# Attention's output summed as 64 by 375 beside the queries, and picked places of two tiles moved to PSUM, in a one-core audio tower on Trainium2

## The reference

```python
q = (x @ Wq).reshape(b, n, HEADS, DIM) * DIM ** (-0.5)
kv_scores, indices = _pk(x, Wq_pk, pk_keys)
k = jnp.einsum('bnhk,bnhkd->bnhd', kv_scores, keys_table[ind])
v = jnp.einsum('bnhk,bnhkd->bnhd', kv_scores, values_table[ind])
sim = jnp.where(causal, jnp.einsum('bihd,bjhd->bhij', q, k), neg)
attn = jax.nn.softmax(sim, axis=-1)
out = jnp.einsum('bhij,bjhd->bhid', attn, v)
return out.transpose(0, 2, 1, 3).reshape(b, n, HEADS * DIM) @ Wo
```

## Time and profile before

| | us |
|---|---|
| median of 3 runs (lowest, highest) | 6795.9 (6795.37, 6803.57) |
| the profiled execution, its own time | 6795.46 |
| its span | 6793.6 |
| PE, busy | 5417.7 |
| POOL, busy | 4478.9 |
| DVE, busy | 3201.8 |
| ACT, busy | 2089.3 |
| mean granted TensorE clock of the span | 0.718 |

### The profile page before, as it was taken

How to read it: one execution, slowest core, us unless ns; L and a number is a source line. 1 busy time by engine, 2 the same in 40 slices (tenths; PEclk the granted TensorE clock), 3 DMA queues, 4 the chain that set the end, 5 groups by cost and what they waited for, 6 DMA issues and landing times.

```text
span 6793.6 us, 88054 instructions
## 1 busy us (share of the span) xinstructions
PE 5417.7 (80%) x24336; PEld 3758.2 (55%) x24336; DVE 3201.8 (47%) x14095; ACT 2089.3 (31%) x4501; POOL 4478.9 (66%) x4574
## 2 busy tenths in 40 slices
PE   2668788887978878787878878787788878788867
PEld 1446556555656556565655656565565656555533
DVE  6534644544464453445454344545534454640156
ACT  0224233332423332232323223232323324232332
POOL 2676767767676776767677676767677676767300
PEclk9667677766767776676777677676767767676767
DMA  1211111111111111111111111111111111111000
GB/s 44 73 51 47 53 45 53 52 46 51 43 53 44 53 52 48 51 44 53 43 53 49 48 53 44 53 43 53 46 51 53 43 53 45 52 47 53 24 22 12
DMA packets 166417, 321.92 MB, mean 47 GB/s; under 512 B 81980, under 2 KB 90772, under 8 KB 165710
## 3 DMA queue, kind: packets, MB, share of 16 engines
q0 software_dynamic: 144384, 295.20, 15.1%
q1 hardware_dynamic: 21166, 20.00, 1.1%
q10 hardware_dynamic: 288, 0.07, 0.0%
HBM read 310.37 MB, written 4.61 MB: 46 GB/s over the span
## 4 chain that ended last, share of the span: by engine, by line
POOL 34%; PE 29%; DVE 15%; issue 15%; ACT 4%; DMA 3%; DVEq 0%; POOLq 0%; SPq 0%; ACTq 0%
POOL store L427 34%; PE gath L613 9%; DMA store<-in,idx_now 3%; PE accu L475 2%; PE dense L467 2%; PE work L636 2%; DVE mx L1359 2%; PE gath L663 1%; PE sims L655 1%; DVE idxf L1299 1%; DVE picks L1295 1%; PE work L595 1%; PE work L690 1%; DVE prob_odd L1356 1%; PE work L648 1%
## 5 line engine op out<-in xcount | busy, mean ns | idle before, releaser
L427 POOL DMA_INDIRECT store<-in,idx_now x4512 | 4457.6, 988 | 1773.8 <-issue 1349.3
L613 PEld LDWEIGHTS gath<-wbd,store 128*128 128x128 f32 (+1 forms) x9024 | 1598.1, 272 | 804.1 <-issue 658.5
L613 PE MATMUL gath<-wbd,store 128*128 128x8 f32 (+1 forms) x9024 | 1591.1, 314 | 508.2 <-DMA store<-in,idx_now 500.1
L887 ACT ACTIVATE past<-dense,edge 128x375 bf16<-128x375 f32 x1024 | 588.2, 574 | 1613.7 <-PE dense L462 1613.4
L475 PE MATMUL accu<-dense_w,store 128*128 128x375 f32 x2048 | 1029.0, 591 | 33.0 <-ACT dense_w L895 33.0
L467 PE MATMUL dense<-parts_f,hot 128*128 128x375 bf16 x3072 | 819.5, 384 | 47.4 <-ACT dense_w L895 45.1
L895 ACT ACTIVATE dense_w<-dense 128x375 f32<-128x375 f32 x1024 | 495.5, 484 | 275.4 <-PE dense L468 260.2
L475 PEld LDWEIGHTS accu<-dense_w,store 128*128 128x128 f32 x2048 | 455.0, 237 | 136.8 <-issue 91.8
L467 PEld LDWEIGHTS dense<-parts_f,hot 128*128 128x128 bf16 x3072 | 317.7, 109 | 366.9 <-issue 274.0
L462 PE MATMUL dense<-ranksT,hot 128*128 128x375 bf16 x1008 | 379.6, 377 | 70.5 <-ACT past L887 70.3
L468 PE MATMUL dense<-past,far 128*128 128x375 bf16 x1024 | 397.6, 388 | 0.0
(11 more groups left out here) (276 smaller groups left out, 6685.3 us busy)
## 6 DMA issues: line engine op xcount, KB each, us to landing
store<-in,idx_now POOLq DMA_INDIRECT x4512, 2.5
x_in<-in SPq DMA_DIRECT2D x16, 187.5 KB
store<-in SPq DMA_DIRECT2D x1, 2048.0 KB, 8.9
queries_kept<-n3T SPq DMA_DIRECT2D x16, 93.8 KB, 2.3
h_saved<-h SPq DMA_DIRECT2D x16, 93.8 KB
store<-queries_kept SPq DMA_DIRECT2D x16, 93.8 KB, 2.3
store<-h_saved SPq DMA_DIRECT2D x16, 93.8 KB
out<-store SPq DMA_DIRECT2D x16, 93.8 KB
```

The source lines that it names most:

```text
L427: nc.gpsimd.indirect_dma_start(rows[0:slots, r * PER + i, :], None, kv_table, bass.IndirectOffsetOnAxis(ap=idx_now[0:slots, at:at + 1], ax ...
L613: last = mm(gath[:, 0, at:at + 8], rows[0:slots, r * PER + i, :], wbd[0:slots, t * GATHERS + n, :], start=True, stop=True)
L887: fn(past[:, n % 2, :], dense[:, 0, 0:S], ACT.Relu, bias=edge[:, 0:1]).then_inc(s["dense_u"], 1)
```

## The change

The mix of attention now has the 64 columns of `vo` as the stationary side and the transposed probabilities as the moving side: three matmuls of 375, 250 and 125 columns that sum into `work[D:128, 0]`, the upper partitions of the bank whose lower ones hold the queries. The blocks of the probabilities are transposed in another order to suit it. At the end ACT copies the 64 by 375 sum to `oT` and PE transposes it back, three blocks of 64 by 125, into `work` bank 1, where DVE's residual add reads it. `last_outputs` moves to `work` bank 1, after `mix(5)`, and PE waits for ACT's copy of it there. The wait for `h2_done` moves from the first row group to `turn_picks` of tile 2. `gath` is then free in attention; `take_inside` could take rows there, but `GROUPS_INSIDE` is eight zeros. Places of tiles 0 and 2 move to PSUM (`sims` bank 0 and `gath`), for which the gradient's results in `sims` bank 0 go to the upper half of `work` and to `work` bank 0. The fill lists take nine groups in `turn` rather than five, and one fewer in three places of `FILL_GRADIENT` and in the last entry of `FILL_SECOND`.

```diff
-FILL_TURN = ((0, 3), (0, 2))
+FILL_TURN = ((0, 5), (0, 4))
-FILL_GRADIENT = ((3, 2), (0, 1), (0, 1), (0, 1), (2, 2))
+FILL_GRADIENT = ((3, 1), (0, 1), (0, 0), (0, 1), (2, 1))
-FILL_SECOND = ((11, 6), (7, 5))
+FILL_SECOND = ((11, 6), (7, 4))
+GROUPS_INSIDE = (0,) * H
...
+        oT = two_q[D:128, 0:S]
-        place_banks = (places_s[:], sims[0:P, 0], places_s[:])
+        place_banks = (sims[0:P, 0], sims[0:P, 0], gath[0:P, 0])
-        PAIRS = [(0, 0, 0), (1, 0, P), (1, 1, 2 * P), (2, 0, 0), (2, 1, P), (2, 2, 2 * P)]
+        BLOCKS = [(0, 0), (0, P), (1, 0), (0, 2 * P), (1, P), (1, 2 * P)]
...
+                if t == 2:
+                    pe.wait_ge(s["h2_done"], b + 1)
...
-                if g == 0 and t == 0:
-                    pe.wait_ge(s["h2_done"], b + 1)
...
-                        last = mm(work[0:P, 0, j * D:(j + 1) * D], kvT[D:128, H - 1, tile(j)], wo_s[D:128, H - 1, :],
+                        last = mm(work[0:P, 1, j * D:(j + 1) * D], kvT[D:128, H - 1, tile(j)], wo_s[D:128, H - 1, :],
...
                 def mix(h):
                     pe.wait_ge(s["pT_done"], b * H + h + 1)
-                    if h == H - 1:
-                        pe.wait_ge(s["vo_done"], b * (NT + 1) + NT + 1)
-                    for c, (i, j, at) in enumerate(PAIRS):
-                        last = mm(gath[0:P, 0, i * D:(i + 1) * D], pT[:, c // 3, at:at + P], vo[:, j, h * D:(h + 1) * D],
-                                  start=(h == 0 and c == 0), stop=(h == H - 1 and c == 5), skip_group_check=True)
+                    for j in range(NT):
+                        last = mm(work[D:128, 0, j * P:S], vo[:, j, h * D:(h + 1) * D], pT[:, min(j, 1), (0, 0, 2 * P)[j]:(S, 2 * P, S)[j]],
+                                  start=(h == 0 and j == 0), stop=(h == H - 1 and j == NT - 1), skip_group_check=True)
...
                     if h + 1 < H:
                         scores(h + 1)
-                    if h + 1 == H - 1:
-                        last_outputs()
                     if h + 2 < H:
                         queries(h + 2)
+                    if following:
+                        take_inside(b + 1, GROUPS_INSIDE[h])
                     dense_steps(b, STEPS_A[h])
                     if h >= 1:
                         mix(h - 1)
+                    if h + 1 == H - 1:
+                        last_outputs()
+                        pe.wait_ge(s["vo_done"], b * (NT + 1) + NT + 1)
...
-                mix(H - 1).then_inc(s["o_mm"], 1)
+                mix(H - 1).then_inc(s["turned_mm"], 1)
+                pe.wait_ge(s["half_done"], b * (H + 1) + H + 1)
+                for t in range(NT):
+                    last = tr(work[0:P, 1, t * D:(t + 1) * D], oT[:, tile(t)], ident[D:128, D:128])
+                last.then_inc(s["o_mm"], 1)
...
-                mm(sims[0:D, 0, 0:S], mlrb[:], n3T[:], start=True, stop=True).then_inc(s["x0_mm"], 1)
+                mm(work[D:128, 0, 0:S], mlrb[:], n3T[:], start=True, stop=True).then_inc(s["x0_mm"], 1)
-                mm(sims[0:D, 0, 0:S], w1T_s[:], dz[:, 1, :], start=True, stop=True).then_inc(s["dx_mm"], 1)
+                mm(work[D:128, 1, 0:S], w1T_s[:], dz[:, 1, :], start=True, stop=True).then_inc(s["dx_mm"], 1)
...
-                    if h + 1 == H - 1:
-                        act.wait_ge(s["vo_mm"], b * (NT + 1) + NT + 1)
-                        nc.scalar.copy(vo[:, :, (H - 1) * D:], work[0:P, 0, 0:NT * D].rearrange("p (j d) -> p j d", d=D)).then_inc(s["vo_done"], 1)
...
                     if h == H - 2 and soften_next is not None:
                         soften(*soften_next)
+                    if h + 1 == H - 1:
+                        act.wait_ge(s["vo_mm"], b * (NT + 1) + NT + 1)
+                        nc.scalar.copy(vo[:, :, (H - 1) * D:], work[0:P, 1, 0:NT * D].rearrange("p (j d) -> p j d", d=D)).then_inc(s["vo_done"], 1)
...
+                act.wait_ge(s["turned_mm"], b + 1)
+                nc.scalar.copy(oT, work[D:128, 0, 0:S]).then_inc(s["half_done"], 1)
...
                 v.tensor_tensor(h2[:].rearrange("p t d -> p (t d)"), h1_now[:].rearrange("p t d -> p (t d)"),
-                                gath[0:P, 0, 0:NT * D], ALU.add).then_inc(s["h2_done"], 1)
+                                work[0:P, 1, 0:NT * D], ALU.add).then_inc(s["h2_done"], 1)
```

More of the change, by code:

```diff
@@ L130, in tower @@
         mlrb = sb("mlrb", [D, D])
-        mblr_s = sb("mblr_s", [D, 1])
+        mblr_s = sb("mblr_s", [128, 1])
         params = sb("params", [D + 1, 2, D])
@@ L626, in fill, with take_inside @@
                         dense_steps(b, 1)
+            def take_inside(b, n):
+                for _ in range(n):
+                    take_group(b, 0, at_group[0])
+                    at_group[0] += 1
             def attention(b, turned_picks, following):
@@ L684, in attention @@
                         mix(h - 1)
+                    if h + 1 == H - 1:
+                        last_outputs()
+                        pe.wait_ge(s["vo_done"], b * (NT + 1) + NT + 1)
                     pe.wait_ge(s["s_norm"], b * H + h + 1)
-                    for c, (i, j, at) in enumerate(PAIRS):
+                    for c, (half, at) in enumerate(BLOCKS):
                         if c == 3:
                             dense_steps(b, STEPS_B[h])
-                            pe.wait_ge(s["half_done"], b * H + h + 1)
-                        last = tr(work[0:P, 1, at:at + P], prob[h % 2][:, c // 3, at:at + P], ident[0:P, 0:P])
+                            pe.wait_ge(s["half_done"], b * (H + 1) + h + 1)
+                        last = tr(work[0:P, 1, c % 3 * P:(c % 3 + 1) * P], prob[h % 2][:, half, at:at + P], ident[0:P, 0:P])
                         if c == 2:
@@ L721, in gradient @@
                     for t in range(NT):
-                        tr(sims[0:P, l, t * D:(t + 1) * D], (x0, x1)[l][0:D, tile(t)], ident[0:D, 0:D])
-                        last = tr(sims[0:P, l, 192 + t * D:192 + (t + 1) * D], dz[:, l, tile(t)], ident[0:D, 0:D])
+                        dst = (work[0:P, 0], sims[0:P, 1])[l]
+                        tr(dst[:, t * D:(t + 1) * D], (x0, x1)[l][0:D, tile(t)], ident[0:D, 0:D])
+                        last = tr(dst[:, 192 + t * D:192 + (t + 1) * D], dz[:, l, tile(t)], ident[0:D, 0:D])
                 last.then_inc(s["t_mm"], 1)
@@ L734, in turn @@
             def turn(b):
+                if isinstance(b, int) and b == 0:
+                    take_inside(0, sum(GROUPS_INSIDE))
                 turn_ranks(b)
@@ L1041, in gradient @@
                 between()
-                fn(sg[:, 2, :], sims[0:D, 0, 0:S], ACT.Sigmoid, bias=mblr_s[:, 0:1]).then_inc(s["alr_done"], 1)
+                fn(sg[:, 2, :], work[D:128, 0, 0:S], ACT.Sigmoid, bias=mblr_s[D:128, 0:1]).then_inc(s["alr_done"], 1)
                 nc.scalar.copy(n3T[:], sims[0:D, 1, 0:S]).then_inc(s["mq_done"], 1)
@@ L1049, in gradient @@
                 act.wait_ge(s["t_mm"], b + 1)
-                for l in range(2):
-                    nc.scalar.copy(xt[:, l, :, 0:D], sims[0:P, l, 0:192].rearrange("p (t d) -> p t d", d=D))
-                    last = nc.scalar.copy(dzt[:, l, :, :], sims[0:P, l, 192:384].rearrange("p (t d) -> p t d", d=D))
+                for l, src in enumerate((work[0:P, 0], sims[0:P, 1])):
+                    nc.scalar.copy(xt[:, l, :, 0:D], src[:, 0:192].rearrange("p (t d) -> p t d", d=D))
+                    last = nc.scalar.copy(dzt[:, l, :, :], src[:, 192:384].rearrange("p (t d) -> p t d", d=D))
                 last.then_inc(s["t_done"], 1)
@@ L1057, in turn @@
             def turn(b):
+                fill(b, 0, sum(GROUPS_INSIDE))
                 keep_ranks(b)
@@ L1415, in gradient @@
                 dve.wait_ge(s["dx_mm"], b + 1)
-                v.tensor_tensor(g2, g2, sims[0:D, 0, 0:S], ALU.add).then_inc(s["g1_done"], 1)
+                v.tensor_tensor(g2, g2, work[D:128, 1, 0:S], ALU.add).then_inc(s["g1_done"], 1)
                 dve.wait_ge(s["g1_done"], b + 1)
```

9 lines of the change are left out of this document (4 added, 5 removed).

## The result

The changed kernel takes 6783.2 us (median of 7, 6776.52 to 6788.48), the kernel before, run beside it, 6803.57 us (median of 7). The ratio is 0.9966, 95% interval 0.995 to 0.9981. The forecast was 6820 us, slower; the sign was wrong, the time lies inside the range. The profiled execution took 6788.39 us (span 6786.6), about the slowest of its seven, and the one of before was about the fastest, so the two traces differ by 7 us only where the medians differ by 20.

The account below looks back on a forecast made before the run. Each 391.8 us cycle was taken as bound by POOL's gathers, then the path through attention to POOL's restart. Terms -82 + 10 + 24 + 42 + 30 = +24 us gave 6820 us, range 6765 to 6856.

Parts of the forecast that it names:

- Part 1, places: Tile 0's places in PSUM stop DVE holding up POOL's gathers: -5.5 us per batch, 15 times, -82 us.
- part (1): Stretch of the cycle from POOL's restart to the end of the last row group: 274.7 us, set by POOL.
- Part 5, fills: Four dense steps instead of three behind the last row group: +1.9 us per batch, 16 times, +30 us.
- The cover of 28.3 us: PE's idle time waiting for rows in part (1), expected to hide the delay from row groups moved ahead, costed at 0.
- Part 4, the end: Copy, three transposes and add between mix(7) and turn_picks of tile 2: +2.6 us per attention, 16 times, +42 us.
- part (4): Stretch of the cycle from attention's last mix to POOL's restart: 6.3 us, on the path, near 9 after the change.
- Parts 2 and 3, mix and head 6: In attention: the wide mix +0.6 us (+10 in all); head 6's wait for ACT's copy +1.5, nothing hides it (+24).
- part (2): Stretch of the cycle from the last row group to the next attention: 9.7 us, near 11.5 after the change.
- forecast (A): Whole kernel: the lengthened tail beats the freed gathers, 6820 us, slower; chance 0.48.
- C: Whole kernel: no change, the two sides cancel, 6795 to 6809 us; chance 0.15.
- rival B: Attention's end: denser mix keeps the clock at 2.4 GHz longer, half of 8.9 us won in 14 attentions, 6758 us; chance 0.2.
- D: PE falls behind in part (1), its 28.3 us of idle time go, slower still at 6865 us; chance 0.12.

Follow-up runs that it names:

- p1_places: The kernel before with only tile 0's places moved to PSUM and the gradient's banks moved out of their way; ratio 0.9876 to the kernel before.
- p2_fills: The kernel before with only the change's four new fill lists; ratio 1.006 to the kernel before.
- p4_undo_places: The changed kernel with the places of tiles 0 and 2 back in SBUF, all else kept; ratio 1.0104 to the kernel before.
- p5_wait: The kernel before with only the last head's projection moved behind mix(5) and PE's wait for its copy; old mix kept; ratio 1.0084 to the kernel before.
- r_after_warm: The changed kernel with ten matmuls that nothing reads added in PE's waits of heads 6 and 7; ratio 0.9899 to the kernel before.
- p8_warm: p1_places with ten matmuls that nothing reads added in PE's waits of heads 6 and 7; ratio 0.9874 to the kernel before.
- r_tail0: p1_places with FILL_SECOND changed so that no dense step stands between a batch's last row group and attention; ratio 0.9819 to the kernel before.
- p9_tail0: The same kernel as r_tail0, timed on an occasion when every kernel took 9.1 to 9.4 ms; ratio 0.9981 to the kernel before.
- p3_mix: The kernel before with the new mix, its end, head 6's wait and the moved wait for h2_done, without places and fills; ratio 1.0086 to the kernel before.
- r_inside3: The changed kernel with three row groups of the next batch summed in heads 5 to 7 of attention, tile 2's places in SBUF; 6434.09 us, ratio 0.9445.
- r_both: r_inside3 with FILL_SECOND changed so that no dense step stands behind the last row group; 6379.72 us, ratio 0.936 to the kernel before.

## Why the prediction was wrong

By its own terms, per cycle, from the means of the two profiles. The forecast's terms make +1.1 us, the measured ones -1.8:

- **Part 1, places: right, 0.9 too small.** Forecast -5.5, measured -6.4 in part (1), and -6.2 in p1_places alone; by ratios 84 to 94 us where 82 stood. One slip: it was counted 15 times, and there are 14 cycles that can gain. The stretch of batch 1's picks lies ahead of the first attention, which starts at 502.5 us in both traces, and the last part (1) had no slow picks already before (268.4 us, after 268.8).
- **Part 5, fills: near.** Forecast +1.9, measured +1.4 here and +2.4 in p2_fills. The cover of 28.3 us held.
- **Part 4, the end: right in the sum, in part by luck.** Forecast +2.6, measured +2.8. In the cycle shown above turn_picks starts 2.0 us behind the last mix's modelled end, where it started 0.2 ahead of it: +2.2. The three transposes took 0.5 us, not 0.8. The rest of the 2.8 is that part (4) too comes in kinds: in the kernel before it was 6.3 us in the cycle that the forecast took, and 8.8 where the turning of the picks ran at 1.2 GHz (rows below, granted clock 0.50).
- **Parts 2 and 3, mix and head 6: the step that failed.** The mechanism was right and the terms were mis-sized: +0.6 and +1.5 were forecast, and attention grew by 0.4 in all. First, at clocks that are alike it grew by 1.3 (p2_fills to p4_undo_places). The wait is 1.1 to 1.2 of that (p5_wait), because head 7 takes 0.65 us back: "nothing hides it" was wrong. The mix is the remaining 0.1 or 0.2: in the middle of attention one head's period rose from 8.75 to 9.05 us and the next one's fell from 9.70 to 9.39. Second, the clock, which the terms left as it was: in the changed kernel 7 of 12 attentions have a tail above 0.75, one had before. The four of them without a dip take 98.3 us, the four with a lower tail and no dip 99.95. 1.7 us in more than half of the cycles are worth some 15 us.

Busy time behind two attentions of the kernel before (columns as above; the clock is 0.78 and 0.50):

```profile
3747.00:3753.00 6.00, 6.00 (x43) 4.99 (x42) 2.07 (x6) 2.86 (x7) 0.00 (x0) 0.78 0.01 1
4136.00:4145.00 9.00, 9.00 (x42) 7.54 (x41) 2.06 (x6) 3.50 (x8) 0.02 (x1) 0.50 0.00 1
```

Against the shorter attentions stands that the changed kernel has more dips (5 for 3). The four terms with their measured sizes make -6.4 + 1.4 + 0.4 + 2.8 = -1.8 us per cycle. When batch 14's attention starts the changed kernel is 16 us ahead; then there is no slow pick left to win on, and it loses 9 of them, some 4 in the last two attentions (92.1 and 88.9 us against 90.8 and 86.3) and 4 in part (2) between them (8.1 against 4.3). That is the 7 us between the traces.

So neither the forecast (A) nor C decided alone: the sum was off by 2.9 us per cycle, 1.7 of them in attention, 0.9 in the places and 0.5 in the fills, less 0.2 at the end; and rival B, which had the faster sign, had its mechanism there in part. It put the gain at half of 8.9 us, 4.45, in every attention; it is 1.7 in seven of twelve, 1.0 on the mean. The rule of the Trainium skill that it leaned on (TensorE: Matmul & The Clock Gate, Part 1: activity of the array releases the gate) agrees with r_after_warm and p8_warm, where added matmuls go with a higher tail (0.82 for 0.77, 0.73 for 0.60). That the denser mix is enough is not borne out by p4_undo_places, whose mix is the wide one and whose tail is 0.60. **Open:** what decides between dip and no dip, and between the two tails. The same matmuls gave both: a place of picks or a fill list switched it, and so did another occasion with the same kernel (r_tail0 and p9_tail0). That the wide mix lifts the tail is not shown, only that the changed kernel and p3_mix have it and p4_undo_places has not.

D fell: PE's waits for rows are still 28.9 us. And the model of the whole, that POOL's stall between its restarts is what the cycle can win, held best: r_inside3 and r_both won 5.5 and 6.4% on the kernel before by it.

## What to carry to other kernels

Move one operand of long elementwise VectorE work to PSUM where a GpSimd queue issues indirect DMAs beside it; it paid here at what one pair of rows had said. Size a wait on the path not at its own place but at the next wait of the same engine, which may take it back. And when the terms sum to a few tenths of a per cent, count the clock's kinds of a stage first, since five attentions of the other kind (some 4.4 us each) weigh as much as the whole change; the large gain lay in what the change made possible, rows inside attention, not in what it did.

## What was not expected of the hardware

- The granted clock falls a second time 20 to 40 us into some attentions (0.76 for 0.88 or more) and in most kernels this costs 3 to 5 us; which attentions it takes changes with edits elsewhere, from none of 13 to seven, and the same kernel had one (r_tail0) and thirteen (p9_tail0, there down to 0.64).
- With ten extra matmuls of no use near its end attention was 2.8 us shorter (r_after_warm), 1.9 where neither kernel had a dip.
- An fp32 mix of 750 columns on 64 stationary ones takes 1.42 us at the full clock, 384 columns in six matmuls 1.26: twice the columns for 13% more time.
- Twice all kernels took 36 to 43% longer, with ACT idle up to 40 us at a time before one line (L901) and no instruction in the trace that releases it.
